# Transformer block: both feed forward layers as three products of operands split in high and low parts

## The chip, the cores and the metric

The kernel runs on one core of one Trainium2 chip. A program for all of the model's layers is launched once, and the time is the device time of that launch in microseconds (us), taken as the median of several runs. A profile is one further execution, recorded instruction by instruction.

The engines are called as the profile calls them: PE is TensorE (matmuls), PEld its weight loads, DVE is VectorE, ACT is ScalarE, POOL is GpSimd and SP is SyncE, which issues the DMAs. "ACTq" and the like are the sequencer of an engine, where it issues an instruction that does no arithmetic.

## The reference

Eight sublayers follow each other on x of 2 x 1024 rows of 256 columns. The change touches one of them, the transformer block (in the program L2_xattn), which computes with y the normalised x of 2 batches of 1024 rows, Z a context of 77 rows for each batch, and a hidden width of 1024:

```python
def _L2_xattn_ref(y, Z, w1, b1, w2, b2, g1, beta1, g2, beta2, g3, beta3):
    sa = attention(y, y, y, causal=True)
    y = layernorm(y + sa, g1, beta1)
    ca = attention(y, Z, Z, causal=False)
    y = layernorm(y + ca, g2, beta2)
    h = jax.nn.relu(jnp.einsum('bsd,df->bsf', y, w1) + b1)
    ff = jnp.einsum('bsf,fd->bsd', h, w2) + b2
    return layernorm(y + ff, g3, beta3)
...
x = x + _L2_xattn_ref(_layernorm(x, axis=-1), ctx_1024, L2_xattn_w1, ...)
```

All operands are fp32. The two feed forward layers are the two lines with `w1` and `w2`.

## The kernel before, in words

`program` runs its stages one after the other, with a barrier of all engines at each end: narrow attention, fp8 product, wide attention, top-2 experts, the transformer block, choice experts, narrow attention, int8 feed forward.

`transformer_block` (L1599) cuts the 16 tiles of 128 rows into 8 units of 2 tiles, which alternate between the two batches (`unit(a)`), so that a later unit attends over more keys: 256 keys at most for units 0 and 1, 1024 for units 6 and 7. Each engine has its own queue, written out by hand as a loop of rounds `it`. In a round three units are under way: `a = it` in self attention, `c = it - 1` in attention over the context, `f = it - 2` in the feed forward, and a fourth, `g = it - 3`, in the last normalisation. Engines meet through counting semaphores. An engine takes its queue strictly in order, so an instruction that waits holds up everything behind it.

TensorE's round (L1809): `scores(a)`; `turn_rows("y2", f)`, the transposes of the rows normalised after the context attention; `turn_first(a + 1)`, the y0 turn; `feed_in(f)`, the product with w1; the y1 turn of c; `turn_probs(a, 0)`; `context_scores(c)`; `turn_probs(a, 1)`; `feed_out(f)`, the product with w2; `turn_context(c)` and `attend_context(c)`; `attend_self(a)`.

ScalarE's round (L1928): rows of y2 and their turned copy `y2T` with scale and shift (`turned_rows`, L1875); the copy of the y0 turn; `rows_self(c)` (L1841); `hidden(f, (0, 1))`, which is relu of PSUM plus b1 into `hid` (L1921); `exponentials(a)` (L1885); `hidden(f, (2, 3))`; the turned copy `y1T` (L1875); copies of the turned probabilities (`turned_probs`, L1895), the context's exponentials, `rows_feed(g)`, `rows_first` of two later units in even rounds, and the turned context probabilities.

VectorE's round (L2089): `maxima(a)`, for each of the two tiles the causal mask, a row maximum and its scaling (L2032, L2034, L2036); `moments` of the feed forward's rows, a chain of some 16 small instructions that gives mean and inverse deviation; in even rounds `first_moments` of two later units; `context_maxima(c)`; `sum_feed(f)` (L2049); `sum_context(c)` (L2056, L2059) and its moments (the last instruction is L2014); `sum_self(a)` (L2071, L2074) and its moments; `next_statistics` (L2086) of an earlier unit.

GpSimd multiplies and adds scales and shifts of 128x512 (L1966 to L1992). SyncE issues all loads at the start of the stage: `w1` at L1691, `w2` at L1693.

PSUM: 4 banks hold the scores. Two banks serve everything that is turned and both halves of `feed_in`: `turn_jobs` lists these jobs in TensorE's order, job r uses bank 4 + r % 2, and `turn_free` makes TensorE wait until ScalarE has taken job r - 2 (`turn_taken`). `feed_in` has four jobs, j = 0 to 3, of four products each, and `hidden` takes them. Two more banks serve the three kinds of output (`out_jobs`, `out_free`). `hid` has one buffer: `hidden(f)` waits for `feed_out(f - 1)`.

```python
def feed_in(f):
    pe.wait_ge(y2T_ready, KC * (f + 1))
    pe.wait_ge(w1_loaded, 32)
...
def feed_out(f):
    pe.wait_ge(w2_loaded, 16)
    pe.wait_ge(turn_taken, turn_at["f1", f, FFC // 2 - 1] + 1)
```

The helper `split_matmul` (L732) is what other stages use for three products: high with high, high with low, low with high (L736 to L738). There ScalarE makes the high part by a copy to fp32r, and VectorE the low part by subtracting (in the choice experts L2570 and L2643 for weights, L2582 and L2648 for hidden rows).

## Time and profile before

| | us |
|---|---|
| median of 3 runs | 1762.41 |
| lowest and highest | 1761.55 and 1776.96 |
| the profiled execution, its own time | 1769.31 |
| its span, first to last instruction | 1767.2 |
| PE busy in the span | 1456.2 (82%) |
| DVE busy | 1107.0 (63%) |
| ACT busy | 747.0 (42%) |
| POOL busy | 641.8 (36%) |
| mean granted clock of TensorE | 0.909 |

All times below count from the start of the span. The transformer block takes the stretch from 826 to 1112 us. The program records an fp32 product as two matmul records and a split one as three. Matmul records overlap, since they are pipelined: the distance between two starts tells the pace, not the duration. The clock is a share of full speed: 1.00 is 2.4 GHz and 0.50 is 1.2 GHz.

### The profile page before, as it was taken

The numbers are of one execution on the slowest core, as the hardware profiler recorded it, in microseconds if no ns is written. First come the engines' busy times: TensorE is split into PE (matmuls) and PEld (weight loads), VectorE is DVE, ScalarE is ACT, GpSimd is POOL, SyncE is SP. The second block draws the span as 40 slices with busy tenths as digits, with TensorE's granted clock in tenths as the row PEclk, the third lists the DMA queues.
The fourth block names the chain that finished last, engine by engine and source line by source line (L and its number), as shares of the span: only waits on it lengthen the run. The fifth ranks groups of instructions, "written<-read, shape, count | busy, mean of one in ns | idle before, by whom it ended". The sixth has DMA issues, their size and how long they took to land. (4 is left out here: it accounts for less than half of the span.)

```text
span 1767.2 us, 25171 instructions
## 1 busy us (share of the span) xinstructions
PE 1456.2 (82%) x9418; PEld 1226.0 (69%) x9418; DVE 1107.0 (63%) x2418; ACT 747.0 (42%) x1295; POOL 641.8 (36%) x435
## 2 busy tenths in 40 slices
PE   6997759998868999994789986638999998599465
PEld 4786658886658999993667765416888887378322
DVE  5776676975446767762566553575666654567568
ACT  3443534442116667761435333103333332254456
POOL 0552225566013555542122222112565655154000
PEclk9899889999869999997799998678999999799788
DMA  5000000000345777754100000412444533300101
GB/s 180 1 1 5 1 1 1 1 1 1 110 144 182 214 218 232 210 155 96 44 1 1 1 1 0 133 36 72 101 96 94 113 75 41 97 1 2 50 0 48
DMA packets 94063, 122.01 MB, mean 69 GB/s; under 512 B 12188, under 2 KB 79159, under 8 KB 93943
## 3 DMA queue, kind: packets, MB, share of 16 engines
q1 hardware_dynamic: 72823, 91.56, 16.0%
q0 software_dynamic: 21120, 28.85, 9.0%
q8 instruction: 76, 1.25, 0.3%
q14 instruction: 44, 0.36, 0.1%
HBM read 94.95 MB, written 25.43 MB: 68 GB/s over the span
## 5 line engine op out<-in xcount | busy, mean ns | idle before, releaser
L1194 POOL DMA_INDIRECT t_total<-t_y,t_index x46 | 99.7, 2167 | 138.4 <-DVE t_y L1315 128.6
L2477 POOL DMA_INDIRECT ch_total<-ch_y,ch_index x64 | 103.9, 1623 | 122.6 <-DVE ch_y L2656 107.7
L3395 POOL TENSOR_TENSOR L_s<-L_s,L_mx 128x1232 f32<-128x1232 f32 x32 | 77.3, 2417 | 141.3 <-DVE L_mx L3457 141.3
L2596 ACT ACTIVATE ch_silu<-ch_ps 128x512 f32<-128x512 f32 x64 | 38.3, 599 | 177.0 <-PE ch_ps L738 175.3
L736 PE MATMUL t_ps<-t_hT_hi,t_w_hi 128*128 128x256 f32 x368 | 106.9, 290 | 7.6 <-DVE t_w_lo L1303 6.0
L736 PE MATMUL ch_ps<-ch_hT_hi,ch_w_hi 128*128 128x512 f32 x256 | 103.9, 406 | 6.9 <-DVE ch_hid L2682 3.6
L736 PE MATMUL t_ps<-t_w_hi,t_act_hi 128*128 128x256 f32 x368 | 105.8, 288 | 0.0
L737 PE MATMUL t_ps<-t_hT_lo,t_w_hi 128*128 128x256 f32 x368 | 105.7, 287 | 0.0
L738 PE MATMUL t_ps<-t_hT_hi,t_w_lo 128*128 128x256 f32 x368 | 105.7, 287 | 0.0
L737 PE MATMUL t_ps<-t_w_lo,t_act_hi 128*128 128x256 f32 x368 | 104.0, 283 | 0.0
L738 PE MATMUL t_ps<-t_w_hi,t_act_lo 128*128 128x256 f32 x368 | 104.0, 283 | 0.0
L738 PE MATMUL ch_ps<-ch_hT_hi,ch_w_lo 128*128 128x512 f32 x256 | 102.6, 401 | 0.0
L737 PE MATMUL ch_ps<-ch_hT_lo,ch_w_hi 128*128 128x512 f32 x256 | 102.5, 400 | 0.0
L2682 DVE TENSOR_TENSOR ch_hid<-ch_silu,ch_ps 128x512 f32<-128x512 f32 x64 | 43.8, 688 | 87.5 <-ACT ch_silu L2596 79.1
L3258 PEld LDWEIGHTS L_ps<-L_vb,L_pT 128*128 128x128 f32 (+1 forms) x640 | 76.7, 197 | 15.8 <-ACT L_pT L3367 15.8
L3258 PE MATMUL L_ps<-L_vb,L_pT 128*128 128x51 f32 (+2 forms) x640 | 80.4, 283 | 8.0 <-ACT L_pT L3367 8.0
L3449 DVE TENSOR_TENSOR L_s<-L_ps,L_neg 128x616 f32<-128x616 f32 x64 | 48.2, 795 | 57.7 <-PE L_ps L3238 57.7
L2467 POOL DMA_INDIRECT ch_hg<-ch_rows,ch_index x64 | 69.6, 1087 | 33.7 <-issue 18.9
L417 PE MATMUL L_ps<-wk_vw,L_pT 128*128 128x256 f32 (+1 forms) x320 | 74.0, 387 | 7.6 <-DVE x L626 5.3
L1327 DVE TENSOR_TENSOR t_act_lo<-t_whole,t_act_hi 128x512 fp32r<-128x512 f32 x92 | 61.7, 689 | 26.5 <-ACT t_whole L1289 23.7
L736 PEld LDWEIGHTS t_ps<-t_hT_hi,t_w_hi 128*128 128x128 f32 x368 | 72.2, 196 | 8.1 <-issue 6.1
L1184 POOL DMA_INDIRECT t_hg<-t_rows,t_index x46 | 49.3, 1072 | 73.2 <-issue 71.1
(524 smaller groups left out, 4432.6 us busy)
## 6 DMA issues: line engine op xcount, KB each, us to landing
t_w_in<-in_L_ffn_w1T SPq DMA_DIRECT2D x23, 1024.0 KB, 4.9
t_w_in<-in_L_ffn_w2T SPq DMA_DIRECT2D x23, 1024.0 KB, 5.6
ch_w_in<-in_L_ffn_w SPq DMA_DIRECT2D x24, 512.0 KB
x<-in_x SPq DMA_DIRECT2D x4, 512.0 KB, 4.8
t_total<-x SPq DMA_DIRECT2D x1, 2048.0 KB
t_rows<-t2d_h SPq DMA_DIRECT2D x1, 2048.0 KB
x<-t_total SPq DMA_DIRECT2D x1, 2048.0 KB, 8.2
tb_w<-in_L_xattn_w SPq DMA_DIRECT2D x2, 1024.0 KB, 12.0
```

The costliest lines, as they stand in the source:

```text
L417: ins = nc.tensor.matmul(ps[:, 7, 0:D], pT[0:rows, n % 2, f, :], vw[0:rows, b, f, :], start=(f == 0), stop=(f == FC - 1))
L736: nc.tensor.matmul(out, sh, mh, start=start, stop=False)
L737: nc.tensor.matmul(out, sh, ml, start=False, stop=False)
L738: return nc.tensor.matmul(out, sl, mh, start=False, stop=stop)
L1184: nc.gpsimd.indirect_dma_start(out=hg[:, j % 3, u, :], out_offset=None, in_=rows, in_offset=bass.IndirectOffsetOnAxis(ap=index[:, 2 * j + ...
L1194: nc.gpsimd.indirect_dma_start(out=total, out_offset=bass.IndirectOffsetOnAxis(ap=index[:, 2 * j + u:2 * j + u + 1], axis=0), in_=y[:, j % ...
L1327: nc.vector.tensor_tensor(act_lo[:, j % 2, 2 * q:2 * q + 2, :], whole[:, q % 2], act_hi[:, j % 2, 2 * q:2 * q + 2, :].bitcast(F32), ALU.su ...
L2467: nc.gpsimd.indirect_dma_start(out=hg[:, s % 3, u, :], out_offset=None, in_=rows, in_offset=at(s, u)).then_inc(gathered[s % 3], 16)
L2477: nc.gpsimd.indirect_dma_start(out=total, out_offset=at(s, u), in_=y[:, s % 2, u, :], in_offset=None, compute_op=ALU.add).then_inc(added[s ...
L3258: ins = nc.tensor.matmul(ps_o()[:, h0 * HEAD:h1 * HEAD], pT[0:rows, n % 2, f, :], vb[0:rows, b, f, 0:(h1 - h0) * HEAD], start=(f == 0), st ...
L3395: nc.gpsimd.tensor_tensor(s[:, n % G], s[:, n % G], spread(mx[:, n % G, :], 2, [P, H, KEYS]), ALU.subtract).then_inc(shifted, 1)
L3449: nc.vector.tensor_tensor(s[:, n % G, c * 8:(c + 1) * 8, :].rearrange("p (j i) n -> p j i n", i=2), ps[:, 0:BANDS, c * 2 * KEYS:(c + 1) * ...
```

## The change

Each of the two products is made of three fp32r products by `split_matmul`. The weights are split once: ScalarE's `weight_hi` makes the high parts of w1 in round 0 and of w2 in round 1, two pieces of 1024 columns each, ahead of the y1 rows and of `turned_probs`, and waits there for the loads; VectorE's `weight_lo` makes the low parts in the same rounds, ahead of `first_moments`. For each unit ScalarE copies y2T (512 columns) into its high part right after it is turned, and each pair of hidden chunks (512 columns) after `hidden`, two before the exponentials and two before the y1 rows. VectorE makes the remainders: `rows_rest` behind `maxima`, `hidden_rest` behind the feed forward's moments and behind `first_moments`. `feed_in` waits for the remainder of y2T and for w1's, `feed_out` for the hidden remainders and w2's. Nothing is taken away but the waits that these replace. All other products of the stage stay as they are.

```diff
--- before.py
+++ after.py
@@ -1616,6 +1616,10 @@
         y1T, y2T = sb("y1T", [P, KC, DUO * P]), sb("y2T", [P, KC, DUO * P])
         cs, pc, pcT = sb("cs", [P, DUO, KEYS]), sb("pc", [P, DUO, KEYS]), sb("pcT", [KEYS, DUO, P])
         hid = sb("hid", [P, FFC, DUO * P])
+        w1_hi, w1_lo = sb("w1_hi", w1.shape, F32R), sb("w1_lo", w1.shape, F32R)
+        w2_hi, w2_lo = sb("w2_hi", w2.shape, F32R), sb("w2_lo", w2.shape, F32R)
+        hid_hi, hid_lo = sb("hid_hi", hid.shape, F32R), sb("hid_lo", hid.shape, F32R)
+        y2T_hi, y2T_lo = sb("y2T_hi", y2T.shape, F32R), sb("y2T_lo", y2T.shape, F32R)
         st, mv, pad = sb("st", [P, 2 * DUO, 6]), sb("mv", [P, 2 * DUO, 2]), sb("pad", [P, 1])
         var, tmp = sb("var", [P, 2 * DUO]), sb("tmp", [P, 2 * DUO])
         rstd, shift = sb("rstd", [P, 4, 2, 2 * DUO]), sb("shift", [P, 4, 2, 2 * DUO])
@@ -1633,6 +1637,9 @@
         beta_ready, y1_ready, y2b_ready, x_added = sem("beta_ready"), sem("y1_ready"), sem("y2b_ready"), sem("x_added")
         dve_chain, pool_chain = sem("dve_chain"), sem("pool_chain")
         next_ready = sem("next_ready")
+        w_hi_ready, w1_lo_ready, w2_lo_ready = sem("w_hi"), sem("w1_lo"), sem("w2_lo")
+        hid_hi_ready, hid_lo_ready = sem("hid_hi"), sem("hid_lo")
+        y2T_hi_ready, y2T_lo_ready = sem("y2T_hi"), sem("y2T_lo")
         block = ctx.enter_context(nc.Block())
 
         def unit(a):
@@ -1784,25 +1791,27 @@
                 ins.then_inc(out_psum, 1)
 
             def feed_in(f):
-                pe.wait_ge(y2T_ready, KC * (f + 1))
-                pe.wait_ge(w1_loaded, 32)
+                pe.wait_ge(y2T_lo_ready, f + 1)
+                pe.wait_ge(w1_lo_ready, KC)
                 for j in range(FFC // 2):
                     turn_free("f1", f, j)
                     for half in range(2):
                         for kc in range(KC):
-                            ins = nc.tensor.matmul(in_halves(turn_bank("f1", f, j))[:, half, :],
-                                                   w1[:, kc, (2 * j + half) * P:(2 * j + half + 1) * P], y2T[:, kc, :],
-                                                   start=(kc == 0), stop=(kc == KC - 1))
+                            cs = slice((2 * j + half) * P, (2 * j + half + 1) * P)
+                            ins = split_matmul(nc, in_halves(turn_bank("f1", f, j))[:, half, :],
+                                               (w1_hi[:, kc, cs], w1_lo[:, kc, cs]), (y2T_hi[:, kc, :], y2T_lo[:, kc, :]),
+                                               start=(kc == 0), stop=(kc == KC - 1))
                     ins.then_inc(turn_psum, 1)
 
             def feed_out(f):
-                pe.wait_ge(w2_loaded, 16)
-                pe.wait_ge(turn_taken, turn_at["f1", f, FFC // 2 - 1] + 1)
+                pe.wait_ge(w2_lo_ready, 2)
+                pe.wait_ge(hid_lo_ready, FFC // 2 * (f + 1))
                 out_free("feed", f)
                 for u in range(DUO):
                     for c in range(FFC):
-                        ins = nc.tensor.matmul(out_bank("feed", f)[:, u, :], hid[:, c, u * P:(u + 1) * P], w2[:, c, :],
-                                               start=(c == 0), stop=(c == FFC - 1))
+                        us = slice(u * P, (u + 1) * P)
+                        ins = split_matmul(nc, out_bank("feed", f)[:, u, :], (hid_hi[:, c, us], hid_lo[:, c, us]),
+                                           (w2_hi[:, c, :], w2_lo[:, c, :]), start=(c == 0), stop=(c == FFC - 1))
                 ins.then_inc(out_psum, 1)
 
             turn_first(0)
@@ -1922,6 +1931,19 @@
                                                    ACT.Relu, bias=b1[:, 2 * j + half:2 * j + half + 1])
                     ins.then_inc(turn_taken, 1)
 
+            def weight_hi(part):
+                if part < KC:
+                    act.wait_ge(w1_loaded, 32)
+                    nc.scalar.copy(w1_hi[:, part, :], w1[:, part, :]).then_inc(w_hi_ready, 1)
+                else:
+                    act.wait_ge(w2_loaded, 16)
+                    cs = slice((part - KC) * FFC // 2, (part - KC + 1) * FFC // 2)
+                    nc.scalar.copy(w2_hi[:, cs, :], w2[:, cs, :]).then_inc(w_hi_ready, 1)
+
+            def hidden_hi(f, j):
+                act.wait_ge(turn_taken, turn_at["f1", f, j] + 1)
+                nc.scalar.copy(hid_hi[:, 2 * j:2 * j + 2, :], hid[:, 2 * j:2 * j + 2, :]).then_inc(hid_hi_ready, 1)
+
             rows_first(0)
             rows_first(1)
             turned_first(0)
@@ -1930,16 +1952,24 @@
                 if 0 <= f < UNITS:
                     rows_context(f)
                     turned_rows("y2", f, y2T, y2T_ready, 2)
+                    nc.scalar.copy(y2T_hi[:], y2T[:]).then_inc(y2T_hi_ready, 1)
                 if a + 1 < UNITS:
                     turned_first(a + 1)
                 if 0 <= c < UNITS:
                     rows_self(c)
                 if 0 <= f < UNITS:
                     hidden(f, (0, 1))
+                    hidden_hi(f, 0)
+                    hidden_hi(f, 1)
                 if a < UNITS:
                     exponentials(a)
                 if 0 <= f < UNITS:
                     hidden(f, (2, 3))
+                    hidden_hi(f, 2)
+                    hidden_hi(f, 3)
+                if it < 2:
+                    weight_hi(2 * it)
+                    weight_hi(2 * it + 1)
                 if 0 <= c < UNITS:
                     turned_rows("y1", c, y1T, y1T_ready, 0)
                 if a < UNITS:
@@ -2085,16 +2115,47 @@
                     t = b * BT + t0 + u
                     nc.vector.bn_stats(k.st[:, t, :], k.x[:, t, :]).then_inc(next_ready, 1)
 
+            def weight_lo(part):
+                dve.wait_ge(w_hi_ready, part + 1)
+                if part < KC:
+                    nc.vector.tensor_tensor(w1_lo[:, part, :], w1[:, part, :], w1_hi[:, part, :].bitcast(F32), ALU.subtract
+                                            ).then_inc(w1_lo_ready, 1)
+                else:
+                    cs = slice((part - KC) * FFC // 2, (part - KC + 1) * FFC // 2)
+                    nc.vector.tensor_tensor(w2_lo[:, cs, :], w2[:, cs, :], w2_hi[:, cs, :].bitcast(F32), ALU.subtract
+                                            ).then_inc(w2_lo_ready, 1)
+
+            def rows_rest(f):
+                dve.wait_ge(y2T_hi_ready, f + 1)
+                nc.vector.tensor_tensor(y2T_lo[:], y2T[:], y2T_hi[:].bitcast(F32), ALU.subtract).then_inc(y2T_lo_ready, 1)
+
+            def hidden_rest(f, j):
+                dve.wait_ge(hid_hi_ready, FFC // 2 * f + j + 1)
+                cs = slice(2 * j, 2 * j + 2)
+                nc.vector.tensor_tensor(hid_lo[:, cs, :], hid[:, cs, :], hid_hi[:, cs, :].bitcast(F32), ALU.subtract
+                                        ).then_inc(hid_lo_ready, 1)
+
             first_moments(1)
             for it in range(UNITS + 3):
                 a, c, f, g = it, it - 1, it - 2, it - 3
                 if a < UNITS:
                     maxima(a)
+                if 0 <= f < UNITS:
+                    rows_rest(f)
                 if 0 <= g:
                     dve.wait_ge(out_taken, out_at["feed", g] + 1)
                     moments(3, g + 1, [r3[:, g % 2, u, :] for u in range(DUO)])
+                if it < 2:
+                    weight_lo(2 * it)
+                    weight_lo(2 * it + 1)
+                if 0 <= f < UNITS:
+                    hidden_rest(f, 0)
+                    hidden_rest(f, 1)
                 if a % 2 == 0 and a + 2 < UNITS:
                     first_moments(a // 2 + 2)
+                if 0 <= f < UNITS:
+                    hidden_rest(f, 2)
+                    hidden_rest(f, 3)
                 if 0 <= c < UNITS:
                     context_maxima(c)
                 if 0 <= f < UNITS:
```

## Rows read from the trace of the kernel before

**Rows 1.** Windows: us, busy time of each engine (instructions), granted clock, DMA share, GB/s.

```profile
867.00:1055.00 188.00, 170.96 (x802) 135.26 (x802) 104.22 (x437) 82.75 (x199) 48.70 (x39) 1.00 0.00 1
```

**Rows 2.** Timeline, PE, transformer stage: start, us, line, out<-in, records [idle before <-releaser].

```profile
867.60 3.69 PE L1793 MATMUL tb_ps<-tb_y2T,tb_w 128*128 128x256 f32 x16 [0.87 <-ACTq L1878]
...
886.80 1.10 PE L1782 MATMUL tb_ps<-tb_ctx_rows,tb_pcT 77*128 77x256 f32 x4 [0.55 <-ACT tb_pcT L1912]
...
895.90 3.69 PE L1793 MATMUL tb_ps<-tb_y2T,tb_w 128*128 128x256 f32 x16 [0.87 <-ACTq L1878]
...
991.27 7.14 PE L1793 MATMUL tb_ps<-tb_y2T,tb_w 128*128 128x256 f32 x32 [0.87 <-ACTq L1878]
998.80 0.63 PE L1720 MATMUL tb_ps<-ident,tb_n 128*128 128x128 f32 x4 [0.38 <-ACT tb_hid L1921]
...
1003.40 7.07 PE L1804 MATMUL tb_ps<-tb_w,tb_hid 128*128 128x256 f32 x32
...
1061.64 3.72 PE L1793 MATMUL tb_ps<-tb_y2T,tb_w 128*128 128x256 f32 x16 [1.86 <-ACT tb_hid L1921]
...
1083.23 1.12 PE L1720 MATMUL tb_ps<-ident,tb_n 128*128 128x128 f32 x4 [6.10 <-ACT tb_n L1841]
1085.52 8.84 PE L1793 MATMUL tb_ps<-tb_y2T,tb_w 128*128 128x256 f32 x32 [1.17 <-ACT tb_y2T L1875]
```

**Rows 3.** Timeline, DVE, transformer stage.

```profile
872.09 0.15 DVE L2036 TENSOR_SCALAR tb_nmx<-tb_mx 128x1 f32<-128x1 f32 x1
...
888.04 0.17 DVE L2056 RECIPROCAL tb_rden<-tb_cden 128x2 f32<-128x2 f32 x1 [1.20 <-PE tb_ps L1782]
...
900.65 0.15 DVE L2036 TENSOR_SCALAR tb_nmx<-tb_mx 128x1 f32<-128x1 f32 x1
...
1027.47 0.15 DVE L2036 TENSOR_SCALAR tb_nmx<-tb_mx 128x1 f32<-128x1 f32 x1
...
1059.69 0.75 DVE L2086 BATCH_NORM_STATS2 st<-x 128x6 f32<-128x256 f32 x2
```

**Rows 4.** Timeline, PE, two neighbouring records of a split product, top-2 experts.

```profile
639.85 0.28 PE L738 MATMUL t_ps<-t_hT_hi,t_w_lo 128*128 128x256 f32 x1
639.97 0.28 PE L736 MATMUL t_ps<-t_hT_hi,t_w_hi 128*128 128x256 f32 x1
```

**Rows 5.** Instructions by line, choice experts: count, ns min/median/max, first and last start, form.

```profile
L2570 ACT CAST ch_w_hi<-ch_w_in x24: 1029/1049/1053, 1175.7 to 1453.7; 128x1024 fp32r<-128x1024 f32 x24
...
L2582 ACT CAST ch_hid_hi<-ch_hid x64: 609/613/625, 1208.8 to 1487.7; 128x512 fp32r<-128x512 f32 x64
...
L2643 DVE TENSOR_TENSOR ch_w_lo<-ch_w_in,ch_w_hi x24: 1217/1219/1222, 1186.4 to 1458.6; 128x1024 fp32r<-128x1024 f32 x24
...
L2648 DVE TENSOR_TENSOR ch_hid_lo<-ch_hid,ch_hid_hi x64: 684/685/724, 1209.6 to 1488.3; 128x512 fp32r<-128x512 f32 x64
```

**Rows 6.** Timeline, ACT, the round of unit 6.

```profile
995.00 0.84 ACT L1921 ACTIVATE tb_hid<-tb_ps,tb_b 128x256 f32<-128x256 f32 x2 [0.80 <-PE tb_ps L1793]
...
999.53 1.02 ACT L1875 ACTIVATE tb_y1T<-tb_ps,tb_turned 128x256 f32<-128x256 f32 x2
```

**Rows 7.** The stage's start: timeline, landing time of tb_w, and a window.

```profile
833.97 0.39 SPq L1691 DMA_DIRECT2D tb_w<-in_L_xattn_w  x1
...
837.27 1.40 DVE L2004 BATCH_NORM_STATS2 tb_st<-x 128x6 f32<-128x256 f32 x4
...
844.04 0.17 DVE L2071 RECIPROCAL tb_rden<-tb_den 128x2 f32<-128x2 f32 x1 [1.94 <-PE tb_ps L1756]
...
DMA to landing us min/median/max: 12.0/12.0/12.0
...
842.00:844.00 2.00, 2.00 (x7) 1.63 (x6) 0.10 (x1) 1.87 (x4) 0.00 (x0) 0.50 1.07 344
```

**Rows 8.** Choice experts: a PE row after a gap, and a window just behind it.

```profile
1218.12 0.50 PE L736 MATMUL ch_ps<-ch_hT_hi,ch_w_hi 128*128 128x512 f32 x1 [3.36 <-DVE ch_hT_lo L2638]
...
1219.00:1220.00 1.00, 1.00 (x4) 0.72 (x3) 1.00 (x2) 0.00 (x0) 0.00 (x0) 0.50 0.00 0
```

## Prediction

> **What bounds the kernel now.** I read the windows first, then the transformer stage on each engine in order of time, then the costs of the same kinds of instruction in the stages beside it. The stage lasts from 826 to 1112 us. In its middle, 867 to 1055, TensorE is busy 171 of 188 us at full clock [rows 1]. So by shares TensorE bounds the middle, and a cheaper product should help.
>
> The order of time says something else. Every round has one gap before the first feed forward product: in the round of unit 3 TensorE starts the context product at 886.80 and feed_in at 895.90; in that of unit 6 feed_in starts at 991.27, the y1 turn at 998.80, feed_out at 1003.40 [rows 2]. VectorE meanwhile is a serial chain of small instructions: in the round of unit 3 it takes up the context result at 888.04 and ends its last row maximum at 900.65 + 0.15 = 900.80 [rows 3], 4.9 us after feed_in had begun. Today nobody on TensorE needs that maximum before feed_in is over. The stage is thus a ring of TensorE, ScalarE and VectorE with about equal laps, and what counts is which queue a new step stands in.
>
> **Products.** An fp32 product of 128x256 is two records; 32 records (16 products) take 7.1 us including the drain, about 427 ns a product without it [rows 2]. The split one is three records 120 ns apart [rows 4], 360 ns. So 67 ns less, 1.07 us for each layer of a unit, 17.1 us in 8 units if all of it showed. The Trainium skill (FP8 and Floating Point Precision, TensorE Precision Notes) says that true fp32 takes four passes through the array; three of four would save a quarter, by the 6.83 us of 16 products 1.7 us a layer and 27 in all, and the forecast would come out 10 lower, at 1801. The trace differs: its three records cost 360 of 427 ns, so I take 17.1.
>
> **The new steps.** A copy of 128x512 into the high part takes 0.613 us on ScalarE, a remainder 0.685 on VectorE; for 1024 columns 1.049 and 1.219 [rows 5]. Per unit that is five of each: 3.07 us on ScalarE, 3.43 on VectorE. Both have idle time enough; the price is in the places.
>
> *Start of feed_in.* It now waits for y2T_lo, and rows_rest stands in VectorE's queue behind maxima, which stands behind sum_context, sum_self and next_statistics. In the round of unit 3 the maxima end at 900.80, rows_rest adds 0.7 and a semaphore 0.1: start 901.5 against 895.90, 5.6 us later. Queued behind the waiting instruction on TensorE are feed_in and all of the round; it has only the y0 turn to do before. The later units have larger score products, which close the gap. The second maxima end in the rounds of units 2 to 7 at 872.24, 900.80, 930.06, 960.73, 993.01, 1027.62 (six L2036 rows, first and last shown [rows 3]); feed_in starts there at 867.60, 895.90, 926.07, 957.82, 991.27, 1026.87 (eight first L1793 rows with 1056.06 and 1085.52, first and last shown [rows 2]). With 0.75 us added that is 5.4, 5.6, 4.7, 3.7, 2.5 and 1.5 us. Round 8 has no maxima but sum_self and next_statistics, the latter from 1059.69 to 1060.44 [rows 3]: start 1061.15, so 5.1. In round 9 only the copy and the remainder lie in the way: 1.4. Sum 29.9. The VectorE chain itself doesn't shrink, since it starts from the context product. Bounds: if the maxima could end a microsecond sooner, 22; if a step of the chain is stretched by a microsecond in each round, 37.
>
> *Inside feed_in.* ScalarE runs hidden 0 and 1, then two copies, the exponentials, hidden 2 and 3, two copies, and only then the y1 turn's result. In unit 6 today hidden 1 runs from 995.00 to 995.84, 4.57 us after feed_in's start, and the y1 rows begin at 999.53, at +8.26 [rows 6]. After: a group j of four products, 12 records, takes 1.44 us, so hidden 1 ends at +4.0, 0.55 sooner; four copies add 2.45: the y1 rows begin at +10.15, 1.9 later. TensorE, done with feed_in at +5.8, waits for its bank until hidden 2 has been taken, about +8. Feed_out follows the y1 rows as today. The same count gives 1.9 for each of rounds 4 to 7, and 0.4 and 0.3 for rounds 2 and 3, where today rows_self holds ScalarE back and won't any more. Round 8 has no exponentials and gains 1.9; round 9 pays 0.8 for the last copy and remainder. Sum 7.2. The remainders are not late: in a round with first_moments hidden_rest 2 and 3 end at about +12.3 (0.7 for each behind 4.3 of moments, two remainders and 4.8 of first_moments), feed_out is due at +13.5. Bounds 3 and 13.
>
> *Feed_out.* It ends 1.07 earlier in every unit and the context product follows it: -8.5. The same 1.07 of feed_in is already in its own count.
>
> *The weights, rounds 0 and 1.* w1 is issued at 833.97 and the landing shown is 12.0 us, so 846.0 for it; at 344 GB/s (842 to 844) its megabyte could be in 3 us before the other one, at 843 [rows 7]. I take 845. Today nobody waits for it before 867. Now ScalarE waits for it ahead of turned_probs(0), and VectorE ahead of first_moments, which started at 837.27 and lasted 4.8 us, and sum_self, which started at 844.04 [rows 7]. Two copies reach 847.1, the second remainder 848.6, first_moments 853.4: sum_self 9.3 us later, and with it rows_self and all of round 1. In round 1 two more copies, 2.1 us, stand between the exponentials and the y1 rows, which are waited for. Sum 11.4, bounds 7.5 and 13. The remainders there fit into VectorE's wait before context_maxima. The DMAs themselves do not move.
>
> *Clock.* With feed_in 5 us late TensorE has gaps of about 6 us with four turns in them. After a gap of 6.10 us the granted clock was half, and feed_in took 8.84 us for 7.14 [rows 2]; after one of 3.36 us it stood at 0.50 in the window from 1219, behind the first products [rows 8]. I count 1.7 us for each of rounds 2 to 5 and 8: 8.5; none at the low end, 17 if the new wait of 2.4 us after feed_in keeps it down. The Trainium skill (TensorE: Matmul & The Clock Gate, Why this matters for your kernels) asks for short idle gaps between bursts, or the clock is halved. By that rule this change makes its own cold starts; the trace agrees in both gaps.
>
> **Sum.** +29.9 + 7.2 - 8.5 + 11.4 + 8.5 = +48.5 us. Against the profiled execution, 1769.3 us with a span of 1767.2, that is 1818; it lies 6.9 above the median of the runs, 1762.4, and from that the forecast is 1811. Nothing outside the stage is touched, and the stage ends in barriers, so all of it shows.
>
> **Rivals.**
> *Products decide.* If TensorE's 171 of 188 us is the true bound and the other two engines catch up, feed_in starts when y2T's parts are ready (+1.4) and the -17.1 shows against 3 or so of late copies and a ramp of little: 1748. For it: the busy share. Against: maxima end after feed_in's start in all six rounds, and VectorE is one queue. It needs VectorE's chain to be 5 us shorter.
> *Half hidden.* The waits in the middle come, but weights land in time (7.5), the clock holds, and steps I took as serial overlap, taking the first two terms to 14: +13, 1775. For it: each term has some slack by ScalarE's many short idle times. Against: I have read no slack in the VectorE chain.
> *Queues without the clock.* As forecast without the 8.5 us: 1802. For: after a gap of 1.86 us in round 8, 16 records still took 3.72 us, the pace of full clock [rows 2]. Against: the gaps here are three times as long.
> *Cold through the round.* The clock doesn't come back within feed_in, since its products are followed by a wait: another 8.5 and some remainders late for feed_out (3): 1822.
> *Doesn't do what it says.* If fp32r products ran at fp32's speed they would be 213 ns apart, 16 x 3 of them 10.2 us a layer where 5.76 is counted, 71 us more in 16 layers: 1882. The rows of the neighbouring stage speak against it.
>
> **How the numbers follow.** Forecast with clock 0.45, queues without clock 0.25, cold through 0.18, half hidden 0.07, products decide 0.03, other slower ones 0.02. Below 1788 lies most of half hidden and products decide; above 1830 little of cold through. Range 1788 to 1830. A measurement of this kernel tells about 1% from no change (its three runs span 1761.6 to 1777.0), that is 1745 to 1780. Faster by more 0.02, within it 0.06, slower by more 0.92.
>
> **What would show it.** The remainder of y2T starts right behind the last L2036 in each round, and feed_in right behind it, with idle time put down to VectorE; six to eight periods between feed_in starts of 31 to 38 us instead of 28.3 to 35.6; 48 records in 5.8 us in feed_out; the first y1 turn waiting for hidden; sum_self(0) around 853; a granted clock under 1.00 in slices of the middle. The forecast is wrong if feed_in starts before the maxima end, if the middle stays at clock 1.00, or if the stage ends before 1130.

## Result, and the profile after

| | before | after |
|---|---|---|
| median, us | 1761.98 | 1826.57 |
| lowest and highest | 1761.37 and 1776.96 | 1822.59 and 1828.97 |
| the profiled execution, its own time | 1769.31 | 1827.02 |
| its span | 1767.2 | 1824.9 |
| mean granted clock | 0.909 | 0.888 |
| length of the transformer stage | 288.4 | 350.3 |

The change makes the kernel slower, by a ratio of 1.0344 [1.0309, 1.0379]. The direction and the range (1788 to 1830) held. The size was too small: 48.5 us forecast, 64.6 by the medians and 61.8 in the stage itself.

The stages ahead of this one differ from execution to execution: the stage begins at 826.0 in the profile of before, at 815.5 in that of after, and between 806.7 and 827.6 in the experiments. So the length of the stage, from its first `tb_st<-x` row on DVE to the `ct_filler` row on POOL behind it, compares kernels more finely than the medians. I cut it at three starts on PE that the rounds have in common: the context product (C), feed_in (F) and feed_out (O). Every length is that of one profiled execution of its kernel. How far it would repeat was not measured, but C to F agrees within 0.3 us in the six kernels that keep the old feed_in.

| sum over the rounds, us | stage | ramp (to first C) | C to F (8) | F to O (8) | O to C (7) | last O to end |
|---|---|---|---|---|---|---|
| before | 288.4 | 31.3 | 90.7 | 92.4 | 54.9 | 19.1 |
| after | 350.3 | 40.1 | 121.9 | 115.4 | 53.4 | 19.5 |
| difference | +61.8 | +8.8 | +31.2 | +23.0 | -1.5 | +0.4 |

Windows of after, the first one as in [rows 1], then two of the round of unit 6: feed_in to feed_out, and feed_out to the context product. Columns as there.

```profile
867.00:1055.00 188.00, 144.13 (x801) 126.02 (x802) 100.91 (x383) 79.01 (x186) 39.19 (x30) 0.84 0.00 1
1024.90:1042.02 17.12, 13.86 (x76) 12.97 (x76) 7.21 (x24) 9.98 (x22) 2.57 (x2) 0.70 0.00 0
1042.02:1049.75 7.73, 7.18 (x52) 6.98 (x51) 0.63 (x1) 2.80 (x9) 3.84 (x3) 0.86 0.01 2
```

TensorE was busy 171 of 188 us at clock 1.00 in [rows 1]. Now it is busy 144 of 188 at 0.84, although each product takes fewer cycles. So the stage got longer by waiting and by a slower clock, not by more work.

PE's timeline in the rounds of units 3 and 6, to set beside [rows 2] (the 48 records of a product stand one by one, so only a few are shown):

```profile
900.31 0.66 PE L1727 MATMUL tb_ps<-ident,tb_n 128*128 128x128 f32 x4
900.80 0.60 PE L1718 MATMUL tb_ps<-ident,tb_y 128*128 128x128 f32 x4
908.09 0.58 PE L736 MATMUL tb_ps<-tb_y2T_hi,tb_w_hi 128*128 128x256 f32 x1 [6.68 <-DVE tb_y2T_lo L2130]
...
910.60 0.41 PE L738 MATMUL tb_ps<-tb_y2T_hi,tb_w_lo 128*128 128x256 f32 x1
910.82 0.41 PE L736 MATMUL tb_ps<-tb_y2T_hi,tb_w_hi 128*128 128x256 f32 x1
...
912.39 0.28 PE L736 MATMUL tb_ps<-tb_y2T_hi,tb_w_hi 128*128 128x256 f32 x1
912.51 0.28 PE L737 MATMUL tb_ps<-tb_y2T_lo,tb_w_hi 128*128 128x256 f32 x1
...
1024.90 0.58 PE L736 MATMUL tb_ps<-tb_y2T_hi,tb_w_hi 128*128 128x256 f32 x1 [3.26 <-DVE tb_y2T_lo L2130]
...
1035.27 0.63 PE L1727 MATMUL tb_ps<-ident,tb_n 128*128 128x128 f32 x4 [1.89 <-ACT tb_hid L1930]
...
1037.90 0.90 PE L1752 MATMUL tb_ps<-ident,tb_p 128*128 128x128 f32 x3 [1.28 <-ACTq L1887]
...
1042.02 0.56 PE L736 MATMUL tb_ps<-tb_w_hi,tb_hid_hi 128*128 128x256 f32 x1
1042.38 0.41 PE L737 MATMUL tb_ps<-tb_w_lo,tb_hid_hi 128*128 128x256 f32 x1
```

In unit 3 the turns end at 901.4 and then TensorE stands for 6.68 us. Feed_in starts 14.91 after the context product at 893.18; before it was 9.10. Its first records come 0.21 to 0.22 us apart (910.60 to 910.82 is one pair), at a granted clock of 0.50 (window from 908.5 to 910.8), the later ones 0.12. I call a start at the slow pace cold. In unit 6 feed_in starts cold, is followed by waits of 1.89 and 1.28 us, and feed_out begins at the slow pace again.

What DVE does meanwhile in unit 3, to set beside [rows 3]:

```profile
894.41 0.17 DVE L2086 RECIPROCAL tb_rden<-tb_cden 128x2 f32<-128x2 f32 x1 [1.21 <-PE tb_ps L1789]
...
904.77 0.16 DVE L2044 SCALAR_TENSOR_TENSOR tb_shift<-tb_mv,tb_rstd 128x2 f32<-128x2 f32 x1
904.97 0.30 DVE L2062 TENSOR_TENSOR tb_ps<-tb_ps,tb_after 128x128 f32<-128x128 f32 x1
...
907.01 0.15 DVE L2066 TENSOR_SCALAR tb_nmx<-tb_mx 128x1 f32<-128x1 f32 x1
907.08 0.95 DVE L2130 TENSOR_TENSOR tb_y2T_lo<-tb_y2T,tb_y2T_hi 128x512 fp32r<-128x512 f32 x1
907.95 0.74 DVE L2034 BATCH_NORM_STATS2 tb_st<-tb_r 128x6 f32<-128x256 f32 x2
```

VectorE has no gap from the context result at 894.41 to the remainder at 907.08. The last maximum ends 12.75 us after the context result was taken up, the same as before (888.04 to 900.80 [rows 3]).

The waits of the stage, longest first among those that concern the change (engine, what waited, what ended the wait: us in total, times, longest):

```profile
DVE tb_hid_lo L2135 <- ACT tb_hid_hi L1945: 39.4, 14, 7.0
PE tb_ps L736 <- DVE tb_y2T_lo L2130: 39.4, 8, 6.7
...
PE tb_ps L1727 <- ACT tb_hid L1930: 9.1, 6, 1.9
...
DVE tb_w_lo L2121 <- ACT tb_w_hi L1937: 7.1, 1, 7.1
...
PE tb_ps L1752 <- ACTq L1887: 5.1, 4, 1.3
```

Eight waits for the remainder of y2T, 39.4 us in all, lie on TensorE's path. The waits for the hidden copies lie on DVE and cost next to nothing: feed_out follows the turns ahead of it without a gap in rounds 2 to 8, and only in round 9, where no turns stand between, does PE stand for 2.8 us before it.

The costs of the new instructions, as in [rows 5] (count, ns min/median/max):

```profile
L1945 ACT CAST tb_hid_hi<-tb_hid x32: 617/628/672, 877.6 to 1144.7; 128x512 fp32r<-128x512 f32 x32
...
L2130 DVE TENSOR_TENSOR tb_y2T_lo<-tb_y2T,tb_y2T_hi x8: 675/776/1752, 870.4 to 1134.8; 128x512 fp32r<-128x512 f32 x8
...
L2135 DVE TENSOR_TENSOR tb_hid_lo<-tb_hid,tb_hid_hi x32: 682/688/693, 878.2 to 1145.4; 128x512 fp32r<-128x512 f32 x32
```

And the ramp, ACT and DVE, to set beside [rows 7] (this stage begins 10.6 us earlier than that one):

```profile
832.80 1.99 ACT L1937 CAST tb_w_hi<-tb_w 128x1024 fp32r<-128x1024 f32 x2 [3.59 <-DMA tb_b<-in_L_xattn_b]
```

```profile
833.88 2.36 DVE L2121 TENSOR_TENSOR tb_w_lo<-tb_w,tb_w_hi 128x1024 fp32r<-128x1024 f32 x2 [7.10 <-ACT tb_w_hi L1937]
...
840.59 0.17 DVE L2101 RECIPROCAL tb_rden<-tb_den 128x2 f32<-128x2 f32 x1
```

The copies wait for the two transfers that count on `w1_loaded`, w1 and its bias b1; the profile puts the end of the wait down to b1's. Both are there at 832.80, 17.35 us into the stage, and sum_self(0) starts at 25.1; before it was 18.0.

So three questions were open. Is the term of 31 us the place of the new wait alone? How much of the rest is the clock? And does the cheaper product pay anything? The experiments take the steps apart one by one. Their table of stages follows here, since all of them are read from it; its columns are those of the table above. Each ratio is to executions of the kernel before that were run beside it.

| sum over the rounds, us | stage | ramp | C to F | F to O | O to C | last O to end | ratio to before [95%] |
|---|---|---|---|---|---|---|---|
| in_only | 330.6 | 38.4 | 121.9 | 94.4 | 56.7 | 19.2 | 1.0241 [1.0188, 1.0295] |
| out_only | 309.9 | 33.1 | 90.4 | 110.6 | 56.3 | 19.5 | 1.0128 [1.0066, 1.0189] |
| plain_products | 358.3 | 40.2 | 121.9 | 117.4 | 59.7 | 19.2 | 1.0411 [1.0348, 1.0474] |
| fill | 335.5 | 40.2 | 123.0 | 99.9 | 52.9 | 19.5 | 1.0292 [1.0248, 1.0337] |
| out_fill | 297.8 | 33.4 | 90.4 | 108.7 | 47.4 | 18.0 | 1.0068 [1.0036, 1.0100] |
| weights_late | 339.9 | 31.7 | 121.9 | 113.0 | 53.9 | 19.5 | 1.0273 [1.0230, 1.0315] |
| rest_pool | 333.3 | 40.4 | 106.3 | 112.7 | 54.1 | 19.8 | 1.0259 [1.0218, 1.0300] |
| out_pool | 301.8 | 31.7 | 90.4 | 106.2 | 55.5 | 18.0 | 1.0098 [1.0064, 1.0132] |
| out_pool2 | 292.5 | 31.7 | 90.4 | 100.0 | 50.9 | 19.5 | 1.0003 [0.9975, 1.0031] |
| mended2 | 312.2 | 31.7 | 107.5 | 99.5 | 54.0 | 19.5 | 1.0145 [1.0105, 1.0184] |
| out_pool3 | 291.0 | 31.7 | 90.4 | 103.4 | 47.4 | 18.0 | 0.9987 [0.9964, 1.0009] |

### The profile page after: what moved, and what is told of

Its sections match the earlier page's. It is cut to its first block and busy times, and to the rows that moved or that the text cites. A ratio compares the mean times of both kernels' runs of the same rounds, so it can differ in the third digit from the quotient of the medians.

```text
span 1824.9 us, 25771 instructions
## 1 busy us (share of the span) xinstructions
PE 1461.0 (80%) x9674; PEld 1245.5 (68%) x9674; DVE 1135.9 (62%) x2462; ACT 770.7 (42%) x1339; POOL 646.0 (35%) x435
## 3 DMA queue, kind: packets, MB, share of 16 engines
q1 hardware_dynamic: 72823, 91.56, 15.6%
q8 instruction: 78, 1.28, 0.3%
## 5 line engine op out<-in xcount | busy, mean ns | idle before, releaser
L736 PE MATMUL tb_ps<-tb_y2T_hi,tb_w_hi 128*128 128x256 f32 x128 | 45.2, 353 | 39.4 <-DVE tb_y2T_lo L2130 39.4
```

Source lines behind the costliest of these rows:

```text
L736: nc.tensor.matmul(out, sh, mh, start=start, stop=False)
```

## The experiments

### One layer at a time: in_only and out_only

in_only keeps the change for feed_in and undoes it for feed_out:

```diff
             def feed_out(f):
-                pe.wait_ge(w2_lo_ready, 2)
-                pe.wait_ge(hid_lo_ready, FFC // 2 * (f + 1))
+                pe.wait_ge(w2_loaded, 16)
+                pe.wait_ge(turn_taken, turn_at["f1", f, FFC // 2 - 1] + 1)
...
-                    hidden_hi(f, 0)
-                    hidden_hi(f, 1)
...
-                if it < 2:
+                if it == 0:
                     weight_hi(2 * it)
                     weight_hi(2 * it + 1)
```

> Only feed_in is split: w1 in round 0, y2T parts, hidden untouched. Queue theory: +7 for w1 ahead of the first probabilities, +31 for feed_in behind the maxima, -3 for shorter products, and half clock in feed_in and partly in feed_out: 1811 (1800 to 1820). Rival, each half carries half: 1794. Rival, the copies of hidden are what costs: under 1780.

Measured: 1809.35 us, stage +42.2. C to F is 121.9, to a tenth what after has: the whole late start belongs to feed_in's operands.

out_only is the mirror image, feed_in in fp32 with its old waits and no `rows_rest`:

```diff
             def feed_in(f):
-                pe.wait_ge(y2T_lo_ready, f + 1)
-                pe.wait_ge(w1_lo_ready, KC)
+                pe.wait_ge(y2T_ready, KC * (f + 1))
+                pe.wait_ge(w1_loaded, 32)
...
-                if 0 <= f < UNITS:
-                    rows_rest(f)
```

> Only feed_out is split: no y2T parts, w1 not split, w2 split in round 1 as in the changed kernel. Queue theory: feed_in starts as before (the 31 us are gone, and the cold starts with them), four copies of 0.61 on ScalarE ahead of the y1 rows cost 2.45 us in rounds 4 to 7 and about 1.5 in the others, w2's copies 2, feed_out gives 8.5 back: +9, 1771 (1765 to 1777), clock 1.00 in the middle. Rival, each half carries half of the loss: 1794. Rival, the saving shows: under 1757.

Measured: 1790.9 us (lowest 1775.9), stage +21.5. C to F is 90.4, as before, so that half held. The time was a miss. PE's timeline behind feed_in in unit 6, and its windows:

```profile
999.97 7.14 PE L1800 MATMUL tb_ps<-tb_y2T,tb_w 128*128 128x256 f32 x32 [0.87 <-ACTq L1886]
1008.53 0.63 PE L1727 MATMUL tb_ps<-ident,tb_n 128*128 128x128 f32 x4 [1.41 <-ACT tb_hid L1929]
1009.26 0.63 PE L1752 MATMUL tb_ps<-ident,tb_p 128*128 128x128 f32 x4
1011.16 0.68 PE L1752 MATMUL tb_ps<-ident,tb_p 128*128 128x128 f32 x3 [1.27 <-ACTq L1886]
```

```profile
1007.00:1011.00 4.00, 1.37 (x9) 0.84 (x8) 2.07 (x4) 4.00 (x10) 0.00 (x0) 1.00 0.00 0
1011.00:1012.00 1.00, 0.72 (x4) 0.38 (x4) 0.00 (x0) 0.77 (x3) 0.00 (x0) 0.72 0.00 0
1012.00:1014.00 2.00, 2.00 (x10) 2.00 (x11) 0.00 (x0) 0.40 (x2) 0.00 (x0) 0.50 0.00 0
```

Feed_in is on time and at full pace here. Behind it TensorE waits 1.41 us for its bank, since ScalarE has two new copies ahead of hidden 2, which frees it (0.38 us before, [rows 2]). It waits 1.27 us once more, for the turned y1 rows, which stand behind all four copies. The clock, still 1.00 until 1011, is 0.50 from 1012. Neither gap is long; between them stand eight small transposes. From the end of feed_in at 1007.11 to the context's scores at 1011.96 TensorE has nothing but these gaps and transposes. I had counted the clock only for the long gap ahead of feed_in.

Together the two halves add 42.2 + 21.5 = 63.7 us to the stage, the whole change 61.8. They are nearly independent.

### The clock: fill and out_fill

fill leaves the change as it is and gives TensorE products to do while it waits for y2T_lo. They are bf16 products of 512 columns; they go into the output bank that feed_out will overwrite, and nobody reads them.

```diff
                 if 0 <= f:
+                    pe.wait_ge(warm_ready, 1)
+                    out_free("feed", f)
+                    keep_busy(nc, ps[:, 6 + out_at["feed", f] % 2, :], warm, {2: 28, 3: 28, 4: 28, 5: 22, 6: 12, 7: 10, 8: 24, 9: 10}[it])
                     feed_in(f)
```

> The changed kernel, with bf16 products of 512 columns that nobody reads put on TensorE ahead of feed_in, 28, 28, 28, 22, 12, 10, 24 and 10 in the rounds of units 2 to 9's place (about as long as the gaps seen there). Clock theory: of the 62 us that the stage lost, 22 come from half clock in feed_in and feed_out; the granted clock is near 1.00 in both and the time falls to 1805 (1799 to 1812). Rival, queues alone: the waits and copies explain it all, the time stays within 3 us of the changed kernel's 1826.6. Rival, too much filler: it delays feed_in and the time rises.

Measured: 1814.51 us, above the range of 1799 to 1812 that I gave; stage 335.5, 14.8 less than after. F to O falls from 115.4 to 99.9. The start of feed_in stays where it was but in round 9, where the filler makes it 1.1 later (C to F 123.0). All eight feed_ins now run at full pace: from the first record to the last 5.7 to 5.8 us each, 46.0 in all, against 61.9 in after. So the slow clock in feed_in costs after some 15.5 us. In the kernel before it costs 1.7 already, in round 9 (8.84 us for 7.14 [rows 2]), which leaves 13.8 for the change, where I had 8.5. O to C hardly moves, 52.9 against 53.4: in fill the clock falls behind feed_in, which I had expected it not to do. It is 0.50 in the window from 877 to 879, ahead of the first feed_out. Its window over the middle:

```profile
867.00:1055.00 188.00, 167.43 (x942) 132.62 (x941) 108.28 (x410) 81.59 (x191) 41.72 (x33) 0.92 0.00 1
```

out_fill tests the other place. It is out_only with five such products behind feed_in and five behind the first turn of probabilities. The first five stand in the first gap of the fence above. The others fill the second gap in rounds 2, 3 and 8. In rounds 4 to 7 that gap lies within `turn_probs(a, 0)`, and they stand right behind it:

```diff
                     feed_in(f)
+                    pe.wait_ge(warm_ready, 1)
+                    out_free("feed", f)
+                    keep_busy(nc, ps[:, 6 + out_at["feed", f] % 2, :], warm, 5)
...
                     turn_probs(a, 0)
+                if 0 <= f < UNITS - 1:
+                    keep_busy(nc, ps[:, 6 + out_at["feed", f] % 2, :], warm, 5)
```

> out_only with 5 bf16 products of 512 columns that nobody reads behind feed_in and 5 more behind the first turned probabilities, where TensorE was idle 1.4 and 1.3 us. Clock theory: the clock fell there although feed_in started on time; with it held the stage falls from 309.9 to about 299 (feed_out start to context start 6.8 instead of 8.1, the turned probabilities at their old pace). Rival, queues alone: 309 to 312.

Measured: stage 297.8, 12.1 less than out_only; median 1775.27. Window over the middle, and PE in a round with the same two waits:

```profile
867.00:1045.00 178.00, 160.63 (x866) 127.23 (x870) 109.34 (x420) 82.21 (x191) 46.62 (x37) 1.00 0.00 1
```

```profile
984.67 1.03 PE L1339 MATMUL tb_ps<-tb_warm 128*128 128x512 bf16 x4
986.04 0.63 PE L1728 MATMUL tb_ps<-ident,tb_n 128*128 128x128 f32 x4 [0.34 <-ACT tb_hid L1935]
...
988.67 0.55 PE L1753 MATMUL tb_ps<-ident,tb_p 128*128 128x128 f32 x3 [1.28 <-ACTq L1892]
989.05 1.24 PE L1339 MATMUL tb_ps<-tb_warm 128*128 128x512 bf16 x5
```

A gap of 1.28 us is still there, the first one is down to 0.34, and the clock stays at 1.00. Which of the two places holds it was not tried apart. Feed_out to context product is now 6.75 to 6.78 us in every round against 7.84 before. That is 1.07 us for a layer of 16 products, the very saving of 67 ns a product. And F to O at full clock is 108.7, 16.3 over before. Of this the fillers themselves take about 1.8: in rounds 5 to 7 the context's scores start 1.24, 1.46 and 1.46 us after the last records of `turn_probs(a, 0)` begin, in out_only 0.80 each time. The remaining 14.5 is what ScalarE's queue and the later remainders cost, without the clock.

### The products alone: plain_products

Both layers are computed in fp32 as before, from the same weights and rows; all splits, remainders and waits of the change stay.

```diff
-                            ins = split_matmul(nc, in_halves(turn_bank("f1", f, j))[:, half, :],
-                                               (w1_hi[:, kc, cs], w1_lo[:, kc, cs]), (y2T_hi[:, kc, :], y2T_lo[:, kc, :]),
-                                               start=(kc == 0), stop=(kc == KC - 1))
+                            ins = nc.tensor.matmul(in_halves(turn_bank("f1", f, j))[:, half, :],
+                                                   w1[:, kc, (2 * j + half) * P:(2 * j + half + 1) * P], y2T[:, kc, :],
+                                                   start=(kc == 0), stop=(kc == KC - 1))
```

> The changed kernel with all its waits, copies and remainders, but both layers as fp32 products of the whole operands. Queue theory: feed_out's 1.07 us a unit are lost again in full, of feed_in only the 0.55 us by which hidden 1 comes sooner, and at half clock the differences double in part: 1840 to 1848. Rival, the split products themselves are what costs (their weight loads): the time falls below 1820. Rival, the products' saving is hidden completely: 1825 to 1829.

Measured: 1834.4 us, ratio 1.0411 [1.0348, 1.0474], a miss: it lies between the 1840 to 1848 that I expected and the 1829 of the rival that hides the saving. The stage is 8.0 longer than in after, of which O to C has 6.3 and F to O only 2.0. So in this surrounding the split product is worth 8 us, half of the 17.1 that its pace offers. Part of what the split saves in feed_in turns into idle time: the six waits of the first y1 turn for its bank take 9.1 us in after and 5.9 here. And the granted clock from the first feed_in to the last context product is 0.89 here against 0.85 in after; that the lower clock eats the rest is argued from these two numbers, not tried.

### The ramp: weights_late

```diff
-                if it < 2:
-                    weight_hi(2 * it)
-                    weight_hi(2 * it + 1)
...
                 if 0 <= c < UNITS:
                     context_turned(c)
+                if it < 2:
+                    weight_hi(2 * it)
+                    weight_hi(2 * it + 1)
```

VectorE's `weight_lo` goes a round later, to rounds 1 and 2.

> The changed kernel with the copies of the weights at the end of ScalarE's rounds 0 and 1, and the remainders one round later on VectorE. Queue theory: the start of the stage to the first context product is 31.3 us as before the change (40.1 in the changed kernel), the rest stays: a stage of 341.5 (339 to 344) against 350.3. Rival, the copies get in the way of rows_self or of round 2: 345 or more.

Measured: 1812.17 us; ramp 31.7 against 40.1 in after and 31.3 before. DVE takes up sum_self(0) 18.4 us into the stage (it starts at 814.73), as before:

```profile
833.09 0.17 DVE L2101 RECIPROCAL tb_rden<-tb_den 128x2 f32<-128x2 f32 x1 [2.27 <-PE tb_ps L1763]
```

All but 0.4 of the ramp's 8.8 us is the place of the weight split. Nothing needs it before round 2, and the rest of the stage does not get longer by putting it off.

### The place of y2T's remainder: rest_pool

GpSimd makes it, right behind the scale and shift of y2b, where it waits some 3 us for the y1 rows:

```diff
                     scale_shift(y2b[:, f % 2], n2[:, f % 2], affine[:, 2, :], beta_b2[:], y2b_ready)
+                    pool.wait_ge(y2T_hi_ready, f + 1)
+                    nc.gpsimd.tensor_tensor(y2T_lo[:], y2T[:], y2T_hi[:].bitcast(F32), ALU.subtract).then_inc(y2T_lo_ready, 1)
...
-                if 0 <= f < UNITS:
-                    rows_rest(f)
```

> The changed kernel with the remainder of y2T made by GpSimd behind its y2b rows instead of by VectorE behind the maxima. Queue theory: feed_in starts 2.0 us later than before the change in each round (0.62 copy, 1.27 GpSimd, 0.1), so context start to feed_in start sums to 107 (121.9 in the changed kernel, 90.7 before); the gap is shorter and so is the time at half clock, another 5: a stage of 330 (325 to 337). Rival, the maxima are needed inside feed_in anyway, and what is gained at its start is lost at the exponentials: 343 or more.

Measured: 1809.81 us; C to F 106.3, 15.6 less than after. Its waits and the cost of the remainder:

```profile
PE tb_ps L736 <- POOL tb_y2T_lo L2011: 23.8, 8, 3.2
```

```profile
L2011 POOL TENSOR_TENSOR tb_y2T_lo<-tb_y2T,tb_y2T_hi x8: 1254/1262/1265, 872.7 to 1122.9; 128x512 fp32r<-128x512 f32 x8
```

The slower engine (1.26 us against 0.69) does it 15.6 us sooner, because it isn't behind the maxima. The other 15.6 of the term stay: 2.0 us a round for a copy on ScalarE, the 1.26 on POOL and the semaphores between. No place I know of takes that out, since turning, copying and subtracting follow each other. A place for the remainder on VectorE ahead of the maxima was not tried; it would have made the chain of maxima longer by 0.7 us.

### Looking for a version that pays: out_pool, out_pool2, out_pool3, mended2

If feed_in can't pay, feed_out alone might: out_only's costs were ScalarE's copies and the ramp. out_pool makes the hidden high parts on GpSimd behind the y1 rows' scale and shift, and splits w2 late.

```diff
+                if 0 <= f < UNITS:
+                    for j in range(FFC // 2):
+                        pool.wait_ge(turn_taken, turn_at["f1", f, j] + 1)
+                        nc.gpsimd.tensor_copy(hid_hi[:, 2 * j:2 * j + 2, :], hid[:, 2 * j:2 * j + 2, :]).then_inc(hid_hi_ready, 1)
```

> Only feed_out split, as in out_only, but the high parts of hidden are copied by GpSimd behind its y1 rows, and w2 is split at ScalarE's end of round 1 and in VectorE's round 2. Queue theory: ScalarE's way to the y1 rows is as before the change, so feed_in start to feed_out start sums to about 92 us over the eight rounds again (110.6 in out_only), the clock stays at 1.00, and feed_out's 8.5 us show: a stage of 280 us (277 to 284) against 288.4, 1753. Rival, GpSimd in VectorE's way: VectorE's chain gets longer by about a microsecond a round and the stage is 285 to 292. Rival, GpSimd's copies come too late for feed_out: over 292.

Measured: stage 301.8, 1780.65 us, a miss, and over the 292 that I had given to copies that come too late. F to O is 16.76, 12.98, 16.00 in rounds 2 to 4 and 11.49, 12.06, 12.08 in rounds 5 to 7. The later rounds are as forecast (before has 11.6 to 12.2), with O to C at 6.78. Rounds 2 and 4 have `first_moments` ahead of the last remainders in DVE's queue; that is the suspect for them, and the next kernel tries it.

out_pool2 moves those two behind what feed_out waits for, GpSimd's copies ahead of the y1 rows, and ScalarE's turned context ahead of `rows_first` (the first of the three edits is shown):

```diff
-                if a % 2 == 0 and a + 2 < UNITS:
-                    first_moments(a // 2 + 2)
...
                     context_maxima(c)
+                if a % 2 == 0 and a + 2 < UNITS:
+                    first_moments(a // 2 + 2)
```

> out_pool with first_moments behind context_maxima on VectorE (where it waits 6 us for feed_out), the turned context ahead of rows_first on ScalarE, and GpSimd's copies ahead of its y1 rows. Queue theory: in out_pool the rounds 5 to 7 had the old way to feed_out (11.5 to 12.1) and a context product 6.78 behind feed_out, and rounds 2 and 4 lost 4 to 5 us to first_moments ahead of the last remainders. With that gone all rounds do as 5 to 7: a stage of 280 to 284 us against 288.4, and a time 0.3 to 0.5% under the kernel before. Rival, other rounds lose by something else (GpSimd in VectorE's way): 288 or more.

Measured: stage 292.5, ratio 1.0003 [0.9975, 1.0031]. Rounds 2 and 4 fall to 12.20 and 13.22 us from F to O, so the three moves together take out most of it; that it is `first_moments` and not the other two was not tried apart. But the time is no better than before's, and 8 to 12 us short of what I expected. In round 3 DVE, POOL and PE do this:

```profile
906.06 5.07 DVE L2133 TENSOR_TENSOR tb_hid_lo<-tb_hid,tb_hid_hi 128x512 fp32r<-128x512 f32 x4
```

```profile
906.63 0.61 POOL L2007 CAST tb_hid_hi<-tb_hid 128x512 fp32r<-128x512 f32 x1 [1.01 <-ACT tb_hid L1929]
907.21 1.71 POOL L1990 TENSOR_TENSOR tb_y<-tb_n,tb_affine 128x512 f32<-128x512 f32 x1
909.00 1.59 POOL L1992 TENSOR_TENSOR tb_y<-tb_y,tb_affine 128x512 f32<-128x512 f32 x1
```

```profile
911.23 0.55 PE L736 MATMUL tb_ps<-tb_w_hi,tb_hid_hi 128*128 128x256 f32 x1 [2.04 <-issue]
```

Four remainders take 5.07 us where four of 0.69 would take 2.8, in the stretch in which POOL copies and then multiplies and adds for the y1 rows; these two are longer too (1.71 and 1.59 us, against 1.27 for each of the pair for y2b at 895.38 and 896.73). Feed_out starts 2.04 us late and at half clock. Over the stage a remainder has these times, in out_pool2 and in out_pool3:

```profile
L2133 DVE TENSOR_TENSOR tb_hid_lo<-tb_hid,tb_hid_hi x32: 679/892/1757, 877.0 to 1099.7; 128x512 fp32r<-128x512 f32 x32
```

```profile
L2142 DVE TENSOR_TENSOR tb_hid_lo<-tb_hid,tb_hid_hi x32: 677/685/1754, 872.6 to 1095.4; 128x512 fp32r<-128x512 f32 x32
```

The Trainium skill (SBUF — State Buffer, Who interferes with whom) says that a VectorE instruction with two inputs in SBUF and a GpSimd instruction that reads SBUF lock each other out, whichever is first. The trace agrees: 0.68 us alone, up to 1.76 beside POOL. In after it touches the main term as well. The remainders of y2T took 0.86, 0.95, 1.75 and 1.39 us in rounds 2 to 5, each beside POOL's work on the y1 rows, and 0.68 or 0.69 in rounds 6 to 9: 2.2 us more in all.

out_pool3 puts the y1 rows between POOL's second and third copy and a few filler products ahead of feed_out:

```diff
+                    pe.wait_ge(warm_ready, 1)
+                    out_free("feed", f)
+                    keep_busy(nc, ps[:, 6 + out_at["feed", f] % 2, :], warm, (2, 4, 4, 0, 0, 0, 3, 6)[f])
                     feed_out(f)
```

> out_pool2 with GpSimd's y1 rows between its second and third copy of hidden, and 2, 4, 4, 0, 0, 0, 3 and 6 products that nobody reads ahead of the eight feed_outs. In out_pool2 the four remainders of round 3 took 5.07 us instead of 2.75 while GpSimd worked on y1, feed_out started 2.2 us late and ran at half clock, 1.1 to 2.2 us more in two rounds. If that is the cause: remainders 2.8 us, feed_out to context product 6.8 in every round, a stage of 286 (283 to 289) and a time 0.1 to 0.3% under the kernel before, at the edge of what is measured. Rival, the filler costs what it saves: 291 or more.

Measured, against 283 to 289 us expected for the stage: 291.0, where the rival of a filler that costs what it saves begins; 1761.10 us (12 executions) against 1763.41 (17), ratio 0.9987 [0.9964, 1.0009]. O to C is 6.76 in all rounds but one, so feed_out pays in full, 7.5 us there and 1.1 at the end. F to O is 11.0 over before and takes it all back. The remainders of round 3 are short now (2.50 us for four), but they start later, since POOL's last two copies stand behind the y1 rows; in rounds 2, 3, 8 and 9 feed_out still starts 0.1 us behind the last of them. In round 4 they are done 1.1 us before feed_out, and four fillers stand in between, so there the filler does cost. In the time no difference from before can be measured.

mended2 has both layers split with everything found so far: late weights, y2T's remainder and the hidden copies on POOL, and out_pool2's order.

> Both layers split as in the change, with every step put where its engine waits: weights late, y2T's remainder and hidden's high parts on GpSimd, first_moments behind context_maxima. Queue theory: feed_in starts 2.0 us late in each round (+15.6), the rest of the round is as before or 0.5 shorter, feed_out gives 7.5 to 8.5 back, with the clock whole: a stage of 292 (288 to 300), where the change had 350. Rival, the products and their number of weight loads are what costs: over 320.

Measured: 1790.68 us, stage 312.2, a miss by 20. C to F is 107.5, as rest_pool has it; F to O is 99.5 and O to C 54.0, and five of its eight feed_outs have records 0.21 us apart, so here too the clock is down. The suspect is feed_in, which starts late in every round. But rounds 2, 4 and 5 have a late feed_in and a feed_out at full pace, so that cause is not shown. It is 38 us better than the change in the stage, and still slower than before.

## Why the prediction was right, and what was mis-sized

The four terms without the clock came to 40.0 us. To read the same from the runs, the clock's part must come out first. F to O loses 15.5 us when the wait for feed_in is filled (after to fill), of which 1.7 were in the kernel before already (round 9): 13.8. O to C is 6.0 over its value at full clock (53.4 against 47.4 in out_fill), and the end 1.5 over (19.5 against 18.0). That is 21.3 for the clock, at least, since in fill the small turns ahead of feed_out still run slow. What is slow there is counted inside feed_in, so that row is an upper value.

| step | forecast | measured | from |
|---|---|---|---|
| start of feed_in | +29.9 | +31.2 | C to F, the same in in_only |
| inside feed_in | +7.2 | +9.1 at most | F to O of fill less before, and round 9's 1.7 |
| feed_out | -8.5 | -8.6 | O to C -7.5 and end -1.1, out_fill less before |
| weights | +11.4 | +8.8 | ramp; gone in weights_late |
| clock | +8.5 | +21.3 at least | as above |
| sum | +48.5 | +61.8 | stage |

The measured column adds up to the stage by the way it is made, so its sum proves nothing; only the split between the rows is a finding.

**Start of feed_in.** Right, in place and size. feed_in follows the remainder, which follows the maxima, in all eight rounds; out_only takes the term away and rest_pool halves it. There is some luck in the size: the 0.7 for a remainder was 0.86 to 1.75 in four rounds, 2.2 us that the prediction did not have, and the whole is still only 1.3 over the forecast.

**Inside feed_in.** Right in kind and near in size. By rounds 2 to 9 fill less before is +1.0, -0.3, +2.3, +2.3, +2.6, +2.6, -2.3 and, without the slow clock of before, +0.8. I had 0.4, 0.3, four times 1.9, -1.9 and +0.8. An estimate from the other side: the 14.5 us of out_fill with fp32 products in feed_in, less 8.5 for eight faster feed_ins, is 6.0.

**Feed_out.** Right where the clock is full. In after O to C shows only 1.5 of it and the end is 0.4 longer, for the clock.

**Weights.** Direction right, 2.6 too high. w1 came 17.4 us into the stage, which is 843.4 on the scale of [rows 7]: my lower bound of 843, not the 845 that I took. sum_self(0) was then 7.1 late instead of 9.3.

**Clock.** This is the step that failed in size: "I count 1.7 us for each of rounds 2 to 5 and 8: 8.5". The mechanism held, and the term measured 21.3 us or more. It was too small in three ways. First, rounds 6 and 7 are slow too, 2.5 and 1.5 us of it. Round 6 is cold after a gap of 3.26 us. Round 7 starts at full pace after 2.63 and falls within feed_in, 16 of its distances being 0.21, so the length of that gap alone doesn't tell where the clock falls. Second, rounds 2 to 5 and 8 lost 2.0 us each on the mean (first to last record 7.1 to 8.2 us against 5.7 in fill), not 1.7. And third, I looked only at the gap that the late start makes. The copies on ScalarE make two more, of 1 to 2 us, between feed_in and feed_out, and with these the clock is gone again when feed_out begins: in after six of the eight feed_outs begin with records 0.21 us apart. out_only showed it without any late feed_in, and out_fill, which closes the first of them and puts work behind the second, undid it. This part is 7.5 us in after. The prediction had named a wait that "keeps it down" as its upper end of 17 us. That end was too low, because it counted feed_in twice over and not feed_out and the turns before it.

**The rivals.** "Cold through the round" (1822) was nearest by the time. Its first half, another 8.5 us of clock, happened and more; its second, remainders late for feed_out, did not. "Queues without the clock" put 40.0 us on the stage; after less its clock is 40.5 at most. "Products decide" is refuted by in_only and out_only, which both lose (its 1748 also leaves out the 1.4 us a round that it grants for y2T's parts), and "half hidden" by C to F, where no microsecond was hidden. "Doesn't do what it says" is refuted by the 0.12 us between records.

**From the stage to the time.** The stage is 13.3 us longer than forecast. The forecast against the profiled execution, 1818, is 9 below its 1827.0; that against the median, 1811, is 15.6 below. The rest is the spread of the other stages, which the change does not touch: in the profiled executions those ahead take 10.6 us less in after and those behind 6.4 more. I had taken "all of it shows" from one execution of before. Of what would show it, one sign was too narrow: the periods between feed_in starts are 31.0 to 41.9 us and not 31 to 38.

## What to carry to other kernels

A cheaper instruction on the busiest engine pays only where its new operands are ready in time: before counting cycles, find the queue that each preparing step will stand in and what stands ahead of it there. A step of 0.7 us behind a serial chain cost 31 us in eight rounds here, and on a slower engine that was free at the time half of that. And when waits on TensorE grow, count the clock for the work behind every one of them, the small turns included, and not just behind the longest.

## What the runs showed of the hardware that I had not expected

- Two gaps of 1.41 and 1.27 us with only eight small transposes between them were followed by a fall of the granted clock from 1.00 to 0.50 within the round (out_only, 1007 to 1014). In [rows 2] gaps of 0.4 to 1.9 us between long products had left it at full pace. With five filler products in the first gap and five behind the second it stayed at 1.00 (out_fill). Whether it is the gaps that count, or that nothing but transposes stood between them, was not tried.
- The same subtraction of 128x512 on DVE took from 0.68 to 1.76 us, the long ones beside work of POOL; POOL's own multiplications went from 1.27 to 1.71 us.
- POOL's copy of 128x512 to fp32r took 0.61 us with DVE idle (out_pool3, round 9, the row below), as fast as ScalarE's 0.62, and up to 1.4 us in out_pool2, where DVE's remainders run beside it. Its subtraction of the same size takes 1.26 against DVE's 0.69.

```profile
1088.78 0.61 POOL L2012 CAST tb_hid_hi<-tb_hid 128x512 fp32r<-128x512 f32 x1 [4.44 <-ACT tb_hid L1933]
```
